# One scaling of the queries moved ahead, and GpSimd's work reordered, in the projection stage of an adaLN block

## The reference, cut to what matters

```python
x = x + gb * _L0_ffn_ref(h, ...)                      # the experts' rows are added to x
h = _layernorm(x, axis=-1) * (1 + ca) + sa
k = short_conv(h @ Wk.T + bk, conv_k)                  # 4 taps along the tokens
q = short_conv(h @ Wq.T + bq, conv_q)
v = short_conv(h @ Wv.T + bv, conv_v)
beta = sigmoid(h @ Wbeta.T + bbeta)
v = silu(v)
k = k / (norm(k) + 1e-06)                              # norm per head of 8 channels
q = q / (norm(q) + 1e-06)
b = beta[..., None] * k
v = beta[..., None] * v
```

## Time and profile before

| | before |
|---|---|
| median of 3 runs | 1977.03 us (1974.11 to 1977.23) |
| the profiled execution: its own time | 1973.72 us |
| its span in the profile | 1971.9 us |
| the projection stage, from the first to the last of VectorE's work in it | 792 to 1003 us of the span |
| granted clock of TensorE in its steady steps | 1.00 of full speed |

### The profile page before, as it was taken

One profiled execution on the slowest core, in us unless ns is written; L12 is line 12 of the kernel. 1 busy time (PEld: TensorE's weight loads), 2 busy tenths in 40 slices (PEclk: granted clock), 3 DMA queues, 4 the chain that ended last, 5 costly groups with the idle time before them and its releaser, 6 DMA issues. The chain is left out here.

```text
span 1971.9 us, 50860 instructions
## 1 busy us (share of the span) xinstructions
PE 1611.2 (82%) x17727; PEld 1253.2 (64%) x17727; DVE 1473.6 (75%) x4099; ACT 1185.5 (60%) x2763; POOL 1093.7 (55%) x1141
## 2 busy tenths in 40 slices
PE   5599999999689697699847777777789607999995
PEld 5478888887577543344415555555578607999994
DVE  7688888888489743699979999999778624555556
ACT  4566666666279821587737888888466504555552
POOL 3378888887000178233247888888637773444440
PEclk8799999999899789799969999999876658999997
DMA  3000000000511123521000000000321112222217
GB/s 120 19 3 4 3 4 4 3 4 3 209 41 41 33 47 43 149 67 43 12 0 1 1 1 1 1 1 1 128 82 50 52 59 66 66 63 66 66 52 262
DMA packets 84954, 92.34 MB, mean 47 GB/s; under 512 B 11696, under 2 KB 69296, under 8 KB 84000
## 3 DMA queue, kind: packets, MB, share of 16 engines
q1 hardware_dynamic: 67840, 62.66, 10.0%
q0 software_dynamic: 14560, 22.24, 4.2%
q10 hardware_dynamic: 2304, 4.20, 0.6%
HBM read 46.14 MB, written 42.91 MB: 45 GB/s over the span
## 5 line engine op out<-in xcount | busy, mean ns | idle before, releaser
L2284 POOL TENSOR_TENSOR delta_A<-delta_A,delta_sW 128x256 f32<-128x256 f32 x256 | 193.6, 756 | 78.6 <-ACT delta_sW L2131 52.1
L2054 PE MATMUL delta_u<-delta_m,tables_sb 128*128 128x256 f32 x512 | 166.1, 406 | 82.0 <-DVE delta_m L2204 82.0
L697 ACT ACTIVATE attn_p_att<-attn_score,attn_mx 128x32 f32<-128x32 f32 (+7 forms) x512 | 150.2, 409 | 133.7 <-DVE attn_mx L759 133.6
L2911 POOL DMA_INDIRECT choice_rows<-ffn_y,ffn_xg x135 | 129.4, 959 | 167.9 <-DVE ffn_y L3018 164.4
L2131 ACT ACTIVATE delta_sW<-delta_W,tables_sb 128x256 f32<-128x256 f32 x256 | 126.6, 506 | 79.1 <-DVE delta_W L2226 75.2
L2054 PEld LDWEIGHTS delta_u<-delta_m,tables_sb 128*128 128x128 f32 x512 | 87.0, 189 | 132.3 <-DVE delta_m L2204 125.6
L2050 PE MATMUL delta_u<-delta_v_own,tables_sb 128*128 128x256 f32 x512 | 153.6, 382 | 9.6 <-DVE xnT L2191 9.6
L2868 POOL DMA_INDIRECT rows<-mix_rows,mix_slot x128 | 125.4, 979 | 47.0 <-issue 39.4
L1327 POOL DMA_INDIRECT exp_rows<-rows,slot_token x32 | 32.6, 1020 | 190.0 <-issue 190.0
L2226 DVE TENSOR_TENSOR delta_W<-delta_W,delta_u 128x128 f32<-128x128 f32 x512 | 133.6, 282 | 4.5
L2213 DVE TENSOR_TENSOR delta_u<-delta_u,delta_prod 128x256 f32<-128x256 f32 x256 | 109.9, 429 | 17.2 <-PE delta_u L2054 3.3
(11 more groups left out here) (397 smaller groups left out, 4693.0 us busy)
## 6 DMA issues: line engine op xcount, KB each, us to landing
ffn_xg<-rows SPq DMA_DIRECT2D x135, 66.0 KB, 1.8
acc<-route_zero SPq DMA_DIRECT2D x10, 832.0 KB, 15.5
comb_rows<-choice_rows SPq DMA_DIRECT2D x32, 256.0 KB, 5.2
rows<-route_rows SPq DMA_DIRECT2D x8, 640.0 KB, 3.6
load_rows<-in_x SPq DMA_DIRECT2D x16, 256.0 KB, 3.7
bT<-acc SPq DMA_DIRECT2D x16, 256.0 KB, 3.9
qT<-acc SPq DMA_DIRECT2D x16, 256.0 KB, 4.5
x_kept<-xT SPq DMA_DIRECT2D x16, 256.0 KB, 2.1
```

The lines of the kernel that those rows point to most:

```text
L697: last = nc.scalar.activation(p_att[:, gr, PAIR_OFF[n]:PAIR_OFF[n] + SLOT * (n + 1)], S[:, gr, c:c + SLOT * (n + 1)], ACT.Exp, bias=mx[:, ...
L2054: nc.tensor.matmul(corrections(h, pp % 2), g.t("same_head"), m1[:, h].rearrange("p t d b -> p (t d b)"), start=False, stop=True).then_inc( ...
L2284: nc.gpsimd.tensor_tensor(A[:, t % 8], A[:, (t - 1) % 8], sW[:, t % RING], ALU.add).then_inc(k.A, 1)
L2911: nc.gpsimd.indirect_dma_start(g.choice_rows, bass.IndirectOffsetOnAxis(xg[:, n % RING, D:D + 1].bitcast(U32), 0), y[:, n % RING, :], None ...
```

## The change

Four things are done at once, all in `project_phase`. TensorE's `widen` is no longer called for keys and then for queries. `widen_most` writes the keys' lengths of both parts and the queries' lengths of part 1, and waits for what both calls waited for, but for the keys of part 0. `widen_last` writes the queries' lengths of part 0 after that wait. VectorE scales the queries of part 1 ahead of those of part 0. GpSimd multiplies the keys by beta ahead of `fix`. And of GpSimd's two sums of rows the one of part 1 waits until `invert` of the next step has made its second instruction (`c.length`), that is, until VectorE comes to its reciprocal.

```diff
-            def widen(i, n):
-                if n == 0:
-                    pe.wait_ge(c.inv_made, i + 1)
-                    if i > 0:
-                        pe.wait_ge(k[0].q_done, i)
-                else:
-                    pe.wait_ge(k[0].k_done, i + 1)
-                pe.wait_ge(k[n].rate, min(i + 2, LAST + 1))
-                if i + 1 > LAST:
-                    pe.wait_ge((k[1].k_done, k[1].q_done)[n], i)
+            def widen(i, parts):
                 for half in halves:
-                    for par in both:
+                    for n, par in parts:
                         last = nc.tensor.matmul(widened(n, par)[:, half * T:(half + 1) * T], pick[group(n, par), half, :],
...
+            def widen_most(i):
+                pe.wait_ge(c.inv_made, i + 1)
+                if i > 0:
+                    pe.wait_ge(k[0].q_done, i)
+                for n in range(2):
+                    pe.wait_ge(k[n].rate, min(i + 2, LAST + 1))
+                if i + 1 > LAST:
+                    pe.wait_ge(k[1].k_done, i)
+                    pe.wait_ge(k[1].q_done, i)
+                widen(i, ((0, 0), (0, 1), (1, 1)))
+
+            def widen_last(i):
+                pe.wait_ge(k[0].k_done, i + 1)
+                widen(i, ((1, 0),))
...
                 if there(i - 1):
-                    widen(i - 1, 0)
+                    widen_most(i - 1)
                 if there(i + 1):
                     channels(i + 1)
                 if there(i - 1):
-                    widen(i - 1, 1)
+                    widen_last(i - 1)
...
                     scale(i - 1, 0, 0)
                     scale(i - 1, 0, 1)
+                    scale(i - 1, 1, 1)
                     scale(i - 1, 1, 0)
-                    scale(i - 1, 1, 1)
...
-            def sum_rows(i):
-                for par in both:
+            def sum_rows(i, pars=both):
+                for par in pars:
...
                     values(i - 1)
+                if there(i - 1):
+                    rates_of_keys(i - 1)
                 if there(i):
                     fix(i)
-                if there(i - 1):
-                    rates_of_keys(i - 1)
                 if 1 <= i + 3 <= LAST:
-                    sum_rows(i + 3)
+                    sum_rows(i + 3, (0,))
+                    if there(i):
+                        pool.wait_ge(c.length, 2 * i + 2)
+                    sum_rows(i + 3, (1,))
```

## The result

The changed kernel takes 1963.82 us (median of 5 runs, 1961.09 to 1964.6) against 1975.78 for the kernel before in the same comparison: a ratio of 0.994, 95% interval 0.9925 to 0.9954. In two later comparisons the changed kernel gave 0.9944 (0.9931 to 0.9957) and 0.9956 (0.9941 to 0.9971). The 12.0 us of the first are more than the 10.0 by which the medians of all runs differ.

The account below looks back on a forecast made before the run. VectorE was taken to set the pace, TensorE not far behind. Terms of 3.05, 3.12, 0.57, 0.6 and 0.6 gave 7.9 us: 1965.8 against the profiled execution, 1969.1 against the median, forecast 1969, range 1965 to 1975.

Parts of the forecast that it names:

- the same sum: All gains in the projection stage: 3.05, 3.12, 0.57, 0.6 and 0.6 give 7.9 us.
- the cases that gain under 4 us: Third widening runs alone (gain 2.9 us, 0.08), row sum blocks convolutions (gain 1.7 us, 0.12), something else returns half (0.07).
- the terms 3.05, 3.12 and 0.57: Five steps of scaling at 0.61 us, four steps of roots at 0.78, and the first roots pass at 0.57.
- the last scaling: After the last reciprocal no scaling follows the queries of part 0, which gains 0.6 us.
- The scaling, 0.61 a step: VectorE's queries of part 1 fill its idle gap while TensorE widens: 0.61 us in each of five steps.
- Three widenings together, free: TensorE's third widening matmul runs beside the other two in its own row group and costs nothing.
- The roots, 0.78 a step: L1827 and L1840 on VectorE no longer collide with GpSimd's row sums: 0.78 us in each of four steps.
- The sum beside the reciprocal, nothing: GpSimd's second row sum beside VectorE's reciprocal costs nothing, 0.3 us before the next convolution; other bound 6.2 us lost.
- The late fix: GpSimd's later fix starts ScalarE's silu 0.4 us later, leaving 0.45 us of slack before the pads.
- The slower rival: The late fix holds up ScalarE, then TensorE; needs a fix 3.5 us later than 879.2; 1981 us, chance 0.05.
- The last passes: In the two last roots passes earlier products free L169: 0.6 us for both together (0 to 1.9).

Follow-up runs that it names:

- the scalings alone: New widenings and scaling order on TensorE and VectorE with GpSimd's old program, against the kernel before: 1974.85 us, ratio 1.0001.
- the kernel with both sums together: The changed kernel with GpSimd's two row sums run at once behind fix, as before the change: 1967.41 us, ratio 0.9969.
- idle waits: The kernel before with five already fulfilled semaphore waits added ahead of GpSimd's second row sum: 1973.97 us, ratio 1.0001.
- the kernel with the sum on the convolutions: The changed kernel with the second row sum released by the end of the reciprocal instead of its start: 1969.87 us, ratio 0.998.
- The kernel with the late second product: The changed kernel, for i of 6 and 7 the keys' product of part 1 also waiting for the reciprocal: 1962.23 us, ratio 0.9945.

## Why the prediction was right and wrong

**Wrong: the base, and a term put at nothing.** Two steps failed. The first is "against the median of the runs, 1977.0, where the same sum gives 1969.1, and I take 1969". The median of three runs was high by 3.3 us: 67 runs of the kernel before have 1973.8, with a standard deviation of 2.1. The second is "The stages around it start anew behind a barrier and should keep their length": the delta stage became 0.73 us shorter. Of the 5.3 us between 1969.1 and the 1963.8 of 16 runs, 3.3 are the base, 0.4 the projection stage, 0.7 the delta stage, and 0.9 lie in no stretch that the profiles pin down.

Neither error alone would have left the range. With the right base and the predicted 7.9 us one gets 1965.9, and with the high base and the measured 10.0 us 1967.0. The low end of 1965 did allow for a base near the profiled execution's and for more gain in the last passes, but for none outside the stage. The sum against the profiled execution, 1965.8, which the prediction states too, was the better one. The chances have a slip of their own: the cases that gain under 4 us have 0.08, 0.12 and 0.07, which is 0.27 and not the 0.18 stated.

**The stage: 8.34 us for 7.9.** Up to the sixth scaling of the keys (144.33 us behind the first convolution before, 137.52 after) 6.81 us were gained; the terms 3.05, 3.12 and 0.57 make 6.74. The rest gained 1.53, where I had 1.2: 0.60 by the last scaling, as predicted, and 0.93 in the two last passes, where I had 0.6.

- *The scaling, 0.61 a step:* right. The starts are 0.60, 0.59 and 0.71 apart, and TensorE's answer is hidden by the scaling of part 1. But it holds only beside the new GpSimd order (the scalings alone gain 0.9 us, and not 3.65).
- *Three widenings together, free:* right. The keys' scaling doesn't wait in the steady steps. It does once near the end, where it did not before, 0.44 us at 978.85.
- *The roots, 0.78 a step:* right; steps of 21.57 us. L1833 takes 0.25 (0.17 alone), L1846 0.30. The wait of "about 0.25" for L1827 was 0.08.
- *The sum beside the reciprocal, nothing:* right; 1.75 us and 3.97 for the convolutions. What I could only bound (0 to 6.2 us) is 0. A sum that comes too late costs 5.2 us, near the upper bound.
- *The late fix:* right; 0.38 us on ScalarE, hidden. The slack ahead of the pads was 0.49 after that, where I had 0.45, and another 1.0 us of delay used it up and still left the step alone. The slower rival, which needed a fix 3.5 us later, did not occur.
- *The last passes:* the direction right, the mechanism half. I expected L169 to be freed, and it was (0.45 and 0.46 for 1.38 and 1.37). I had overlooked that the products also hold L1840 there, 1.00 and 0.45 us: the first stayed and the second grew to 1.20. Of the 0.93 that L169 gained in the first of these passes, 0.44 went into the wait of the keys' scaling. The last pass also differs between executions: in the repetition of the kernel before L1840 took 1.00 and L169 0.42 there.

**Missed: 0.73 us in the delta stage.** "The stages around it start anew behind a barrier and should keep their length" is wrong by that much. The work kept its order; GpSimd's program ahead of it had changed (last section).

**Open.** The means of the runs differ by 9.9 us, and the two stretches that repeat explain 9.1. All five profiles, stretch by stretch in us:

| | before, its repetition | changed, three profiles |
|---|---|---|
| start to the first convolution | 820.80, 819.69 | 821.75, 823.06, 819.26 |
| to the delta stage | 182.30, 182.56 | 173.96, 174.00, 174.00 |
| delta stage | 409.38, 409.43 | 408.65, 408.84, 408.85 |
| `mix_phase` | 222.47, 224.99 | 221.96, 221.47, 220.82 |
| the rest | 336.95, 337.93 | 336.48, 338.63, 338.97 |

`mix_phase` is shorter in all three profiles of the changed kernel, by 2.3 us in the mean, and the first and last stretch of the table together are longer by 1.7, so that the spans differ by 9.7 in the mean. Over all thirteen profiles it takes 222.5 to 225.0 us in the four whose kernels gain nothing in time, and 219.4 to 223.0 in the nine others. The two groups overlap, and no run shows whether the change shortens this stage. TensorE's granted clock may bear on it: over `mix_phase`, as a mean of its two levels, it was 0.62 and 0.61 in the two profiles of the kernel before, and 0.62, 0.64 and 0.64 in those of the changed one. The time of whole runs goes with it too: of 73 runs of the kernel before whose clock is listed, the 17 at 0.907 or less have a mean of 1976.1 us, the 18 at 0.912 or more one of 1972.1.

## What to carry to other kernels

Two engines that share a resource can hide one another's fixes: look where the freed instruction lands, and test the parts together as well as alone, since here 0.9 and 4.7 us of the stage made 8.3. The reciprocal of 1.75 us was a place for GpSimd's sum, which slowed the roots ahead of it and the convolutions behind it, but only with the sum released when the reciprocal starts and not when it ends. And add a sum made from a profile to a base with as many runs as the effect needs: three runs with a spread of 3 us cannot carry a prediction to 2.

## What was not expected of the hardware

**GpSimd's gaps by its place in the program.** In the delta stage GpSimd is idle for 0.43 us at two places, with nothing that releases it there, in every kernel with the added waits (all nine profiles), and never in the kernel before, its repetition, the scalings alone or the kernel with both sums together. Timelines of GpSimd in the changed kernel and in that with idle waits, the first of the two gaps:

```profile
1065.96 0.72 POOL L2293 TENSOR_TENSOR delta_A<-delta_A,delta_sW 128x256 f32<-128x256 f32 x1 [0.17 <-POOL delta_m L2304]
1067.12 2.50 POOL L2293 TENSOR_TENSOR delta_A<-delta_A,delta_sW 128x256 f32<-128x256 f32 x3 [0.43 <-POOL delta_A L2293]
```

```profile
1075.31 2.50 POOL L2289 TENSOR_TENSOR delta_A<-delta_A,delta_sW 128x256 f32<-128x256 f32 x3 [0.43 <-POOL delta_A L2289]
```

Without the gap the four run in one piece, and VectorE's instruction beside them is held. Timelines of GpSimd and of VectorE before, and of VectorE after:

```profile
1073.36 3.33 POOL L2284 TENSOR_TENSOR delta_A<-delta_A,delta_sW 128x256 f32<-128x256 f32 x4 [0.17 <-POOL delta_m L2295]
```

```profile
1076.02 0.95 DVE L2237 TENSOR_TENSOR delta_m<-delta_A,delta_prod 128x256 f32<-128x256 f32 x1
```

```profile
1068.62 0.42 DVE L2246 TENSOR_TENSOR delta_m<-delta_A,delta_prod 128x256 f32<-128x256 f32 x1
```

After the gap VectorE gets in first and needs 0.42 us instead of 0.95. Each of the two gaps saves 0.4 to 0.5 us, and in the changed kernel 0.2 is lost again later. That an idle moment of an engine made the stage shorter is luck, and it does not always show. In the kernel with the sum on the convolutions the same two gaps are there, but the stage takes 409.58 us, for 0.86 is lost ahead of them. Timeline of VectorE there:

```profile
1032.15 0.43 DVE L2222 TENSOR_TENSOR delta_u<-delta_u,delta_prod 128x256 f32<-128x256 f32 x1 [0.66 <-PE delta_u L2063]
...
1033.31 0.43 DVE L2222 TENSOR_TENSOR delta_u<-delta_u,delta_prod 128x256 f32<-128x256 f32 x1 [0.40 <-PE delta_u L2063]
```

VectorE waits for TensorE, whose granted clock between 33 and 36 us behind the start of the stage was 0.85 (the rise from half to full speed falls into it), where it was 1.00 in the kernel before. The kernel with the late second product loses 0.74 us at the same place (0.88), and the second and third profile of the changed kernel 0.3. So the 0.73 us saved are not all there in each execution: 0.54 to 0.73. What makes the gap no run shows. That it comes with the added waits, and not with the moment at which the stage starts, is shown by the idle waits.

**Held instructions of 8 elements.** L1833 handles 128 x 8 numbers in 0.17 us, and took up to 1.17 when GpSimd was in a sum in the steady steps: what it paid went with when it came (0.25, 0.58, 0.91, 1.17), not with its size.

**A reciprocal beside GpSimd.** It reads SBUF at 1.75 us for 256 elements and neither holds GpSimd's addition of two SBUF operands (1.27) nor is held by it, while an integer `TENSOR_SCALAR` of 264 elements is (0.75 to 0.86 for 0.30).
